# Householder columns: VectorE's order within a column, x.Ax summed by itself at 3 and 4 live blocks, the next column's norm made during a panel's update

## The reference

```python
deg = jnp.sum(A, axis=0) + jnp.sum(A, axis=1) - jnp.diagonal(A)
d_inv_sqrt = jnp.where(deg > 0, jax.lax.rsqrt(deg), 0.0)
L = jnp.diag(deg) - A
L_norm = d_inv_sqrt[:, None] * L * d_inv_sqrt[None, :]
_, U = jnp.linalg.eigh(L_norm)
agg = jnp.einsum('mn,bnd->bmd', U.T, features)
```

## Time and profile before

| what | us |
|---|---|
| median of 3 runs | 7037.88 |
| lowest and highest run | 7037.35, 7040.46 |
| span of the profiled execution | 7032.6 |
| stage of 4 live blocks (45 to 749) | 704 |
| stage of 3 live blocks (749 to 1375) | 626 |
| stage of 2 live blocks (1375 to 1959) | 584 |
| stage of 1 live block (1959 to 2510) | 551 |

### The profile page before, as it was taken

How to read it: one execution, slowest core, us unless ns; L and a number is a source line. 1 busy time by engine, 2 the same in 40 slices (tenths; PEclk the granted TensorE clock), 3 DMA queues, 4 the chain that set the end, 5 groups by cost and what they waited for, 6 DMA issues and landing times. The chain is left out here.

```text
span 7032.6 us, 110639 instructions
## 1 busy us (share of the span) xinstructions
PE 5280.7 (75%) x33091; PEld 3792.1 (54%) x33091; DVE 4595.9 (65%) x27972; ACT 2313.6 (33%) x7361; POOL 17.9 (0%) x36
## 2 busy tenths in 40 slices
PE   5777666655555569988999995895574699876899
PEld 4666555555544435545666663563342467544676
DVE  7888888887878753337999999678444333424333
ACT  2222222222222224336778985110020133301333
POOL 0000000000000000000000000000000000000000
PEclk9999999999999999988999997997787799976899
DMA  0000000000000000000000000000010000000000
GB/s 37 2 2 2 2 1 1 1 1 1 1 1 1 1 20 1 0 35 19 6 4 6 6 4 8 1 1 1 1 48 1 12 0 0 9 0 13 0 0 24
DMA packets 23221, 48.24 MB, mean 7 GB/s; under 512 B 5673, under 2 KB 16322, under 8 KB 20930
## 3 DMA queue, kind: packets, MB, share of 16 engines
q1 hardware_dynamic: 22722, 42.40, 1.8%
HBM read 34.00 MB, written 8.39 MB: 6 GB/s over the span
## 5 line engine op out<-in xcount | busy, mean ns | idle before, releaser
L476 PE MATMUL h_M<-h_part,ones 128*128 128x2 f32 x1024 | 300.5, 363 | 576.2 <-DVE h_jd L384 576.2
L476 PEld LDWEIGHTS h_M<-h_part,ones 128*128 128x128 f32 x1024 | 256.4, 311 | 619.9 <-DVE h_jd L384 619.9
L1774 DVE SCALAR_TENSOR_TENSOR f_ACC<-f_yp,f_CG,f_ACC 128x128 f32<-128x128 f32 x1024 | 288.2, 344 | 461.8 <-DVEq L1772 461.8
L1719 PEld LDWEIGHTS f_yp<-f_W,f_hs 128*128 128x128 f32 x4096 | 490.1, 192 | 92.6 <-issue 91.8
L1653 PE MATMUL f_hp<-f_rows,f_W 128*128 128x512 f32 x1024 | 531.5, 601 | 5.1 <-ACT U L1663 3.1
L821 ACT ACTIVATE e_XD<-e_X,e_scal 128x60 f32<-128x60 f32 x2048 | 527.7, 333 | 17.5 <-DVEq L685 15.7
L1750 ACT ACTIVATE f_hs<-f_hp,f_b 128x512 f32<-128x512 f32 x512 | 347.6, 685 | 539.7 <-ACTq L1749 539.7
L471 PEld LDWEIGHTS h_ax<-h_XM,h_parts 128*128 128x128 bf16 x11520 | 508.8, 116 | 0.0
L1709 PE MATMUL f_hp<-f_XT,f_W 128*128 x1024 | 483.7, 600 | 33.0 <-PEq L2003 33.0
L436 ACT ACTIVATE h_VW<-h_v,h_s 128x8 f32<-128x8 f32 (+3 forms) x512 | 154.9, 302 | 1044.6 <-DVE h_s L388 1044.6
L1719 PE MATMUL f_yp<-f_W,f_hs 128*128 128x128 f32 x4096 | 493.5, 275 | 0.0
(11 more groups left out here) (688 smaller groups left out, 11242.6 us busy)
## 6 DMA issues: line engine op xcount, KB each, us to landing
f_S<-in_f_W SPq DMA_DIRECT2D x64, 128.0 KB, 2.4
X<-in_x SPq DMA_DIRECT2D x1, 4096.0 KB, 16.3
f_W<-in_f_W SPq DMA_DIRECT2D x2, 2048.0 KB
spill<-f_xts SPq DMA_DIRECT2D x16, 256.0 KB, 2.0
f_rows<-spill SPq DMA_DIRECT2D x16, 256.0 KB, 2.6
f_W<-in_f_W SPq DMA_DIRECT2D x4, 1024.0 KB
out<-X SPq DMA_DIRECT2D x1, 4096.0 KB, 11.1
h_A<-in_adj SPq DMA_DIRECT2D x1, 1024.0 KB, 5.4
```

What stands on the lines that cost most here:

```text
L476: nc.tensor.matmul(dots, C.ones[:, :], part[:, 2:4], start=True, stop=True).then_inc(dots_out, 1)
L1719: ins = nc.tensor.matmul(yp[:, u % 2, k, :], hs[:, u % 2, c, k * P:(k + 1) * P], W2[:, u * UC + c, :], start=(c == 0), stop=(c == UC - 1))
```

## The change

Three things are changed in `tridiagonalize`, and the column's steps become small functions that are called in an order of their own for wide columns (3 and 4 blocks, `wide_step`) and narrow ones (2 and 1, `narrow_step`).

At 3 and 4 blocks x.pc is no longer one dot. Its part x.Ax is summed straight from the parts of Ax in PSUM (`xax`) and sent to TensorE alone; the rest of it, x.zc, is put together from sums that are already there: the corrections' sums, which are copied out of PSUM (`srs`), their products in pairs (`cross`, `ab`), and one more sum, x times the next column of A. The dot v.pc/2 gets its own accumulator, matmul and PSUM column (`part2`, `dots2`), and the W column that needs it is written in the next column, in front of the sums with V and W. The next x is then two steps: `vm` times the known part less `base`, and on top of that `vm` times the dot.

At 2 and 1 blocks the dots stay as they are and VectorE's instructions are put in another order. In TensorE's queue the corrections' matmul moves: behind half of the groups of Ax (two of four, one of three, one of two), at one block behind all.

From the second panel of a stage on, the first column's norm and reflector are made while TensorE forms the panel's update: `norm_parts`, the root, `signed_norm`, `leading`, `reflector` and `inverses` stand between the copy of the transposed columns and the update of A. The last panel of a stage no longer splits the block that is done with. The matmuls on `tiny` go; the tiny term is added by one more element of x.

```diff
...
+        xax = sb("xax", [P, NB, 3])
+        sums, srs = sb("sums", [P, 2 + 2 * PAIR]), sb("srs", [P, 2 + 2 * PAIR])
+        cross, ab = sb("cross", [P, 2 * PAIR]), sb("ab", [P, 4])
+        part, part2 = sb("part", [P, 4]), sb("part2", [P, 1])
+        ss = sb("s", [P, 2, 16])
-        tiny = sb("tiny", [P, 2])
+        turned, dots, dots2 = M[0:PAIR, NB - 2, :], M[:, 0, 0:2], M[:, 1, 0:1]
...
+            split_sums = L > 2
+            SUM0 = 2 if split_sums else 1
+            ahead = lambda panel: panel in panels and panel > panels[0]
...
+    def norm_parts(done, j):
+        q = j % 2
+        first, x, below = column(q)
+        R_1, R_2 = XM[:, q, live, R1], XM[:, q, live, R2]
+        if j > 0:
+            dve.wait_ge(ch, made["x"])
+        V_.scalar_tensor_tensor(ja[:, ph:NB + 1], XM[:, q, ph:NB + 1, XC], 1.0, XM[:, q, ph:NB + 1, XC], ALU.mult, ALU.mult,
+                                accum_out=part[:, 0:1])
+        if j > 0:
+            dve.wait_ge(masks_in, j)
+        else:
+            dve.wait_ge(mask0, 1)
+            dve.sem_clear(mask0)
+        if L > 1:
+            V_.scalar_tensor_tensor(jb[:, live], x, 1.0, first, ALU.mult, ALU.mult, accum_out=part[:, 1:2]).then_inc(part_in, 1)
+        else:
+            V_.tensor_tensor(part[:, 1:2], x, first, ALU.mult).then_inc(part_in, 1)
+        V_.tensor_tensor(R_1, x, XB[:, q, live, 2 * XC + 1], ALU.subtract).then_inc(ch, 1)
+        r1_made = done.next()
+        V_.scalar_tensor_tensor(prod[:, 0, live], x, 0.0, below, ALU.not_equal, ALU.mult).then_inc(ch, 1)
+        made["nonzero"] = done.next()
+        dve.wait_ge(ch, r1_made)
+        V_.tensor_tensor(R_2, R_1, XB[:, q, live, 2 * R1 + 1], ALU.subtract).then_inc(xb_in, 1)
...
+    def sign_norm(done, j, twice):
+        s = ss[:, j % 2, :]
+        if j > 1:
+            dve.wait_ge(kept, j - 1)
+        dve.wait_ge(ch, twice)
+        V_.tensor_tensor(s[:, 7:8], s[:, 6:7], s[:, 3:4], ALU.mult).then_inc(ch, 1)
+        made["c"] = done.next()
...
+    def pair_sums(done, j):
+        q, J = j % 2, 2 * j
+        first, x, below = column(q)
+        xm = XM[:, q, live, :]
+        if j > 0:
+            dve.wait_ge(ch, made["w"])
+            V_.tensor_tensor(
+                prod[:, SUM0:SUM0 + 2 * J, live].rearrange("p (h j) b -> p h j b", h=2),
+                VW[:, live, 0:J].rearrange("p b j -> p j b").unsqueeze(1).broadcast_to([P, 2, J, L]),
+                xm[:, :, FIRST:XC + 1].rearrange("p b h -> p h b").unsqueeze(2).broadcast_to([P, 2, J, L]),
+                ALU.mult).then_inc(ch, 1)
+            made["nonzero"] = done.next()
+        dve.wait_ge(ch, made["nonzero"])
+        V_.tensor_reduce(sums[:, 0:SUM0 + 2 * J], prod[:, 0:SUM0 + 2 * J, live], AX.X, ALU.add).then_inc(sums_in, 1)
...
+    def update_column(done, j, half_vp):
+        J = 2 * j
+        dve.wait_ge(scaled_out, j + 1)
+        ins = V_.scalar_tensor_tensor(VW[:, live, J + 1:PAIR + J + 1:PAIR - 1], two(VW[:, live, J]), half_vp,
+                                      two(pc[:, live]), ALU.mult, ALU.subtract)
+        if j < PW - 1:
+            ins.then_inc(ch, 1)
+            made["w"] = done.next()
+        else:
+            ins.then_inc(panel_in, 1)
+    def wide_step(done, j, k):
+        q, J = j % 2, 2 * j
+        first, x, below = column(q)
+        if j > 0:
+            dve.wait_ge(dots2_out, j)
+            update_column(done, j - 1, dots2)
+        V_.tensor_tensor(prod[:, 1, live], x, A[:, live, k + 1], ALU.mult).then_inc(ch, 1)
+        made["nonzero"] = done.next()
+        pair_sums(done, j)
+        if j > 0 or not made["ahead"]:
+            signed_norm(done, j)
+            leading(done, j)
+            reflector(done, j)
+            inverses(done, j)
+        dve.wait_ge(sr_out, j + 1)
+        V_.tensor_copy(srs[:, 0:2 + 2 * J], sr[:, 0:2 + 2 * J]).then_inc(ch, 1)
+        held = done.next()
+        dve.wait_ge(ch, held)
+        if j > 0:
+            spread(done, j, srs[:, 2:2 + 2 * J])
+        inverse_c(done, j, srs[:, 0:1])
+        if j > 0:
+            V_.tensor_tensor(
+                cross[:, 0:2 * J].rearrange("p (h i t) -> p h i t", h=2, t=2),
+                srs[:, 2:2 + 2 * J].rearrange("p (h i t) -> p h i t", h=2, t=2)[:, :, :, ::-1],
+                srs[:, 2 + J:2 + 2 * J].rearrange("p (i t) -> p i t", t=2).unsqueeze(1).broadcast_to([P, 2, j, 2]),
+                ALU.mult).then_inc(ch, 1)
+            crossed = done.next()
+        scales(done, j)
+        corrected(done, j)
+        if j > 0:
+            dve.wait_ge(ch, crossed)
+            V_.tensor_reduce(ab[:, 0:2], cross[:, 0:2 * J].rearrange("p (h m) -> p h m", h=2), AX.X, ALU.add).then_inc(ch, 1)
+            added = done.next()
+        scaled_x(done, j)
+        if j > 0:
+            dve.wait_ge(ch, added)
+            V_.tensor_tensor(ab[:, 2:3], ab[:, 0:1], srs[:, 1:2], ALU.add).then_inc(ch, 1)
+            added = done.next()
+        shifted_column(done, j)
+        dve.wait_ge(ax_out, j + 1)
+        V_.scalar_tensor_tensor(xax[:, live, :], ax[:, live, :], 1.0, x.unsqueeze(2).broadcast_to([P, L, 3]), ALU.mult, ALU.mult,
+                                accum_out=part[:, 2:3]).then_inc(part_in, 1)
+        sum_parts(done)
+        if j > 0:
+            dve.wait_ge(ch, added)
+            V_.scalar_tensor_tensor(ab[:, 3:4], ab[:, 2:3], ss[:, q, 7:8], ab[:, 1:2], ALU.mult, ALU.add).then_inc(ch, 1)
+        else:
+            dve.wait_ge(ch, max(held, made["c"]))
+            V_.tensor_tensor(ab[:, 3:4], srs[:, 1:2], ss[:, q, 7:8], ALU.mult).then_inc(ch, 1)
+        rest = done.next()
+        product_column(done)
+        base_column(done, j)
+        dve.wait_ge(ch, made["v"])
+        V_.scalar_tensor_tensor(jd[:, live], vs[:, q, live], 0.5, pc[:, live], ALU.mult, ALU.mult,
+                                accum_out=part2[:, 0:1]).then_inc(part2_in, 1)
+        masked_base(done, j)
+        dve.wait_ge(ch, max(made["base"], made["vm"], rest))
+        V_.scalar_tensor_tensor(base0[:, live], vm[:, live], ab[:, 3:4], base[:, live], ALU.mult, ALU.subtract).then_inc(ch, 1)
+        dve.wait_ge(ch, done.next())
+        dve.wait_ge(dots_out, j + 1)
+        V_.scalar_tensor_tensor(XM[:, 1 - q, live, XC], vm[:, live], dots[:, 0:1], base0[:, live], ALU.mult, ALU.add).then_inc(ch, 1)
+        made["x"] = done.next()
+    def narrow_step(done, j, k):
+        q, J = j % 2, 2 * j
+        first, x, below = column(q)
+        pair_sums(done, j)
+        twice = None
+        if j > 0 or not made["ahead"]:
+            twice = signed_norm(done, j)
+        dve.wait_ge(sr_out, j + 1)
+        if j > 0:
+            spread(done, j, sr[:, 1:1 + 2 * J])
+            sign_norm(done, j, twice)
+        corrected(done, j)
+        dve.wait_ge(ax_out, j + 1)
+        sum_parts(done)
+        if j > 0 or not made["ahead"]:
+            reflector(done, j)
+        shifted_column(done, j)
+        if j > 0 or not made["ahead"]:
+            leading(done, j)
+        product_column(done)
+        if j > 0 or not made["ahead"]:
+            inverses(done, j)
+        dve.wait_ge(ch, max(made["pc"], made["v"]))
+        if L > 1:
+            V_.scalar_tensor_tensor(jc[:, live], x, 1.0, pc[:, live], ALU.mult, ALU.mult, accum_out=part[:, 2:3])
+            V_.scalar_tensor_tensor(jd[:, live], vs[:, q, live], 0.5, pc[:, live], ALU.mult, ALU.mult,
+                                    accum_out=part[:, 3:4]).then_inc(part_in, 1)
+        else:
+            V_.scalar_tensor_tensor(part[:, 3:4], vs[:, q, live], 0.5, pc[:, live], ALU.mult, ALU.mult).then_inc(ch, 1)
+            done.next()
+            V_.tensor_tensor(part[:, 2:3], x, pc[:, live], ALU.mult).then_inc(part_in, 1)
+        inverse_c(done, j, sr[:, 0:1])
+        scales(done, j)
+        base_column(done, j)
+        scaled_x(done, j)
+        masked_base(done, j)
+        dve.wait_ge(ch, max(made["base"], made["vm"]))
+        dve.wait_ge(dots_out, j + 1)
+        V_.scalar_tensor_tensor(XM[:, 1 - q, live, XC], vm[:, live], dots[:, 0:1], base[:, live], ALU.mult, ALU.subtract).then_inc(ch, 1)
+        made["x"] = done.next()
+        update_column(done, j, dots[:, 1:2])
+    done = Count()
+    made["ahead"] = False
+    for panel in panels:
         for j in range(PW):
...
+            if j > 0 or not made["ahead"]:
+                norm_parts(done, j)
+            (wide_step if split_sums else narrow_step)(done, j, panel * PW + j)
+        if split_sums:
+            dve.wait_ge(dots2_out, PW)
+            update_column(done, PW - 1, dots2)
+        dve.wait_ge(ch, made["x"])
         dve.wait_ge(kept, PW)
-        for used in (ch, masks_in, dots_out, sr_out, root_out, ax_out, scaled_out, kept):
+        for used in (ch, masks_in, dots_out, dots2_out, sr_out, root_out, ax_out, scaled_out, kept):
             dve.sem_clear(used)
+        done.restart()
         dve.wait_ge(turn_out, 1)
         dve.sem_clear(turn_out)
```

(109 more changed lines are left out.)

205 lines of the change are left out of this document (81 added, 124 removed).

## The result

The changed kernel takes 7152.2 us (median of 4 runs, 7147.6 to 7154.6) beside 7037.6 (7037.1 to 7040.5) for the kernel before on the same chip: ratio 1.0159, 95% interval 1.0145 to 1.0173. That is 115 us slower, where 7213 was forecast, in a range of 7080 to 7270.

A forecast was written before the change was run, and what follows sets the result against it. No engine was full; a chain through VectorE's in-order queue, with three TensorE round trips per column, was taken as the bound. 95 + 109 - 10 - 16 + 1 - 4 = +175 us gave 7213 us, range 7080 to 7270.

The forecast's parts named there:

- What bounds the wide columns: At 4 and 3 blocks, VectorE's longer in-order list sets the period, no longer the dot: +95 and +109 us.
- The middle of a wide column: Four blocks, j = 14: copy 2.93, spread 3.17, x.Ax 4.67 us behind x; nine steps instead of five, +0.35.
- the price of the copy's dependency: Wide columns: spread waits for the copy of the sums; copy's turn and dependency together +0.40 us at four blocks.
- One with two waits starts 0.10 behind the end of the later: Layout price in us for any VectorE instruction with two waits; one waiting only for its predecessor starts 0.035 behind it.
- The narrow columns: At 2 and 1 blocks, the same instructions in a new VectorE order: -10 and -16 us.
- Boundaries and stage ends: Norm during the update at 28 panel boundaries, with the stages' first columns: +1 us; less splitting at four stage ends: -4.
- The signs of being wrong: x.Ax starting within 0.1 us of Ax's end, small added steps closer than 0.075, or wide stages shrinking.
- The third: Sign of error in the changed profile: VectorE starts the small added steps closer than 0.075 us.
- the faster one: Wide columns: added work fits into VectorE's wait for Ax, so only tails count, -49 us; 6960 us in all; 8%.
- Seven more instructions at a whole dependent pitch: No overlap between VectorE instructions: seven more at 0.19 us in 240 wide columns, +319, 7357 us in all; 3%.

The follow-up runs named there:

- run 1: Changed kernel with the narrow columns' order at all four widths (one matmul for both dots, no copy of the sums): 6988.2 us, ratio 0.9940.
- run 4: Changed kernel with the correction sums at four blocks behind 12 matmuls again instead of 24: 7143.7 us, ratio 1.0163.
- run 6: Changed kernel with the wide columns' product x.Ax moved four places earlier on VectorE: 7152.2 us, ratio 1.0160.
- run 7: Changed kernel with two unused one-element copies added on VectorE in each wide column: 7188.5 us, ratio 1.0214.
- run 3: Changed kernel with wide columns' spread reading the correction sums directly from PSUM, not waiting for the copy, which stays: 7138.8 us, ratio 1.0152.
- run 5: Kernel before the change, with the two waits ahead of c and the two ahead of x each written in the other order: 6985.7 us, ratio 0.9926.
- run 2: Changed kernel with the narrow order at all widths and the first column's norm and reflector made behind the panel's update again: 6991.2 us, ratio 0.9941.
- run 8: Changed kernel with narrow-column instructions in a searched order per width, waits ahead of c and x swapped, four-block sums behind 12 matmuls: 6946.2 us, ratio 0.9870.

## Why the prediction was right, and where it was off

- **What bounds the wide columns.** Right. Run 1 takes the loss away with the list, runs 4 and 6 show that TensorE's order and the dot have no part, run 7 that an instruction more is time more. The size was put too high: +175 forecast, +115 measured.
- **The middle of a wide column.** The copy was put at 2.93 behind x and is at 2.92, spread at 3.17 and is at 3.15, x.Ax at 4.67 and is at 4.61. Run 3 confirms the price of the copy's dependency.
- **The step that failed** is the price "One with two waits starts 0.10 behind the end of the later". The earlier trace rows show 0.11 for c and 0.12 for x, but in both the later one is the wait written second. Where the second is long satisfied, there is no price: run 5. In the changed kernel the last instruction on VectorE comes last, and its wait is the first of the pair. So x follows the combine by 0.03 instead of 0.10: 0.065 in each of 240 wide columns, 16 us of the 25 that were missing (+179 measured, +204 forecast). W, both of whose waits are over, starts 0.09 behind the instruction before it instead of 0.15, but in this column hardly any of that arrives: the product behind it takes 0.58 instead of the 0.54 of the earlier trace rows, and the copy is 0.01 early. The other 0.05 of the column comes in small steps between the copy and x.Ax; the 9 us that are left over all columns are not put down to single steps, and W was not tried by itself.
- **The narrow columns**, likewise, gained 48 instead of 26. At two blocks, j = 3, the masked base is the later one, and TensorE's dot, issued at 1567.23, the earlier:

```profile
1567.23 0.59 PE L714 MATMUL h_M<-h_part,ones 128*128 128x2 f32 x2 [1.16 <-DVE h_jd L577]
...
1567.75 0.15 DVE L471 TENSOR_TENSOR h_base<-h_base,h_XM 128x2 f32<-128x2 f32 x1
...
1567.94 0.23 DVE L590 SCALAR_TENSOR_TENSOR h_XM<-h_vm,h_M,h_base 128x2 f32<-128x2 f32 x1
```

  x starts 0.04 behind the base's end, and the base is the later one in all 240 narrow columns. 0.065 less in each is 16 of the missing 22 us; the other 6 stay open. The corrected price was tried ahead of a result in run 5, on the old order: 542.5, 501.2, 490.8 and 477.5 us laid out, 542.3, 500.0, 486.1 and 473.5 measured.
- **Boundaries and stage ends.** -3 forecast, -5.1 measured, but the parts miss in opposite ways, so the sum is near by luck. The 28 boundaries were put at +1 with the first columns and give -4.2 (-0.48 each at two blocks, where -0.2 was laid out) and +0.7 at the first x; the stage ends were put at -4 for four, and the three that the table has give -0.9. In the narrow order the norm during the update is worth 9 us (run 2). Against the kernel before, boundaries and stage end of 3 and 4 blocks together are 0.9 and 0.7 shorter in the changed kernel, 2.9 and 2.2 in run 1; that the first wide column's longer list takes the difference is argued, not tried.
- **The signs of being wrong.** Two did not come: the wide stages grew, and x.Ax never started within 0.1 us of the end of Ax. The third did, by a hair: `cross` starts 0.07 behind the instruction in front of it, closer than 0.075, so some added steps were cheaper than laid out.
- **The rivals.** x.Ax comes at least 0.62 us after Ax stands, 1.25 in the column shown, so the faster one never got near its condition, and run 6 shows that its gain was not there to be had. Seven more instructions at a whole dependent pitch would have given +319: run 7 shows a third of such a pitch for each.

## What to carry to other kernels

When a wait is taken off the critical chain by adding work to the engine that does the waiting, lay out that engine's whole list first: it gains only as long as the list is shorter than the wait. Where an instruction waits for two semaphores, write the one that comes last first. And compare the changed stretch itself in the two traces, start to start, ahead of the totals: in run 3 the total hid four fifths of a gain that each column shows.

## What the runs showed of the hardware

**The order of two waits is worth 52 us of 7038** (run 5), with the same instructions and the same semaphores.

**Code that nobody touched takes 54 or 73 us.** Some 3.8 ms behind the last x there is a chain of small matmuls with VectorE in between. Its products on TensorE (minimum, median and longest duration in ns, then first and last start), in the kernel before, the changed one and run 3:

```profile
L3016 PE MATMUL g_PM<-g_MM,g_NT x64: 415/421/472, 6293.0 to 6366.4; 128*128 128x64 f32 x64
```

```profile
L3253 PE MATMUL g_PM<-g_MM,g_NT x64: 275/275/470, 6432.7 to 6486.4; 128*128 128x64 f32 x64
```

```profile
L3253 PE MATMUL g_PM<-g_MM,g_NT x64: 418/421/471, 6400.2 to 6473.6; 128*128 128x64 f32 x64
```

Over this stretch the mean granted clock was 0.67 in the kernel before and 0.92 in the changed one; both lie between the two levels (1.2 GHz would be 0.50, 2.4 GHz 1.00), so the one kernel spent more of the stretch at the lower:

```profile
6292.50:6366.50 74.00, 56.99 (x176) 46.70 (x176) 13.51 (x29) 1.28 (x1) 0.00 (x0) 0.67 0.00 0
```

```profile
6432.50:6486.50 54.00, 37.32 (x176) 31.02 (x176) 13.29 (x28) 1.02 (x1) 0.00 (x0) 0.92 0.00 1
```

In the one profiled execution of each, the changed kernel and runs 4, 6 and 7 have 54 us there; the kernel before and runs 1, 2, 3 and 5 have 73, and run 8 has 70. In the 40 us right ahead of it TensorE was busy 32.2 us in the kernel before and 31.6 in the changed one, at a mean clock of 0.87 in both, so little sets them apart. Which of the two it is went with no edit that I can name. A change in the first third of a kernel can so gain or lose 20 us, 0.3%, four milliseconds later, and what decides it stays open.
